# The first wide attention: the maxima's bias and mask come as bf16 tables through one product, and VectorE adds two key tiles for the softmax sums, whose product stands a tick later

## The reference, cut to what matters

```
q = _l2norm(q) * q_scale
k = _l2norm(k) * k_scale
sim = jnp.einsum('bhid,bhjd->bhij', q, k) * ATTN_SCALE
...
sim = sim + dist[None, None] * slopes[None, :, None, None]
...
sim = jnp.where(causal_mask[None, None], neg, sim)
attn = jax.nn.softmax(sim, axis=-1)
out = jnp.einsum('bhij,bhjd->bhid', attn, v)
...
return out @ w_out
```

## Time and profile before

| | us |
|---|---|
| three runs | 2496.67, 2497.49, 2497.55 |
| median | 2497.49 |
| the profiled execution | 2501.75 |
| its span in the profile | 2500.1 |
| TensorE busy in the span | 2348.6 (94%) |
| VectorE busy | 1606.9 (64%) |
| ScalarE busy | 1484.6 (59%) |
| GpSimd busy | 1588.9 (64%) |
| transfers, mean | 33 GB/s |

### The profile page before, as it was taken

One profiled execution on the slowest core, in us unless ns is written; L12 is line 12 of the kernel. 1 busy time (PEld: TensorE's weight loads), 2 busy tenths in 40 slices (PEclk: granted clock), 3 DMA queues, 4 the chain that ended last, 5 costly groups with the idle time before them and its releaser, 6 DMA issues. The chain is left out here.

```text
span 2500.1 us, 61330 instructions
## 1 busy us (share of the span) xinstructions
PE 2348.6 (94%) x23721; PEld 1826.3 (73%) x23721; DVE 1606.9 (64%) x4042; ACT 1484.6 (59%) x2974; POOL 1588.9 (64%) x2537
## 2 busy tenths in 40 slices
PE   6999999999999999988999999999999968799997
PEld 5888888888886556656777787787877757566665
DVE  5666666666664578874445477777777733378786
ACT  5666666666664478864444466666666523377774
POOL 6888888888885364443333277777777732367663
PEclk9999999999999989999999999999999979899999
DMA  8940000000000010001000000000000036100000
GB/s 293 331 142 2 2 2 2 2 2 2 2 2 1 1 47 2 2 2 33 1 1 1 3 4 4 6 6 4 6 6 4 6 100 183 55 10 10 8 4 34
DMA packets 22915, 82.90 MB, mean 33 GB/s; under 512 B 3970, under 2 KB 10883, under 8 KB 21603
## 3 DMA queue, kind: packets, MB, share of 16 engines
q1 hardware_dynamic: 19474, 71.76, 8.9%
q0 software_dynamic: 3152, 7.21, 0.9%
HBM read 71.76 MB, written 46.79 MB: 47 GB/s over the span
## 5 line engine op out<-in xcount | busy, mean ns | idle before, releaser
L978 POOL TENSOR_TENSOR XR<-XR,T 128x256 f32<-128x256 f32 x504 | 368.9, 732 | 36.9 <-DVE T L858 7.3
L722 ACT ACTIVATE P<-ps 128x384 f32<-128x384 f32 (+1 forms) x512 | 250.7, 542 | 179.5 <-PE ps L2755 178.1
L2755 PE MATMUL ps<-P,V 128*64 128x256 f32 (+3 forms) x4096 | 335.0, 349 | 0.8 <-ACT P L722 0.7
L1523 DVE TENSOR_REDUCE bm<-ps 128x3 f32<-128x384 f32 x512 | 260.6, 551 | 54.4 <-PE ps L2755 52.0
L2755 PEld LDWEIGHTS ps<-P,V 128*64 128x64 f32 (+1 forms) x4096 | 186.1, 124 | 123.6 <-issue 47.0
L1463 ACT ACTIVATE P<-ps 128x768 f32<-128x768 f32 x256 | 207.7, 811 | 75.6 <-PE ps L2755 70.3
L889 DVE TENSOR_REDUCE sm<-ps 128x2 f32<-128x512 f32 (+1 forms) x256 | 130.0, 549 | 188.0 <-PE ps L2755 188.0
L1630 POOL TENSOR_SCALAR_AFFINE_SELECT P<-P 128x512 f32<-128x512 f32 x256 | 165.5, 647 | 103.6 <-ACT P L1463 102.0
L991 POOL TENSOR_TENSOR PS<-P 128x256 f32<-128x256 f32 x256 | 181.4, 734 | 70.8 <-ACT P L722 70.5
L2755 PE MATMUL ps<-mk,identb 128*128 128x256 bf16 (+1 forms) x1024 | 204.7, 291 | 12.7 <-DVE bm L1523 8.9
L1012 POOL TENSOR_TENSOR ss<-ss,nhalf 128x16 f32<-128x16 f32 x64 | 188.0, 2938 | 5.3
(11 more groups left out here) (315 smaller groups left out, 6838.5 us busy)
## 6 DMA issues: line engine op xcount, KB each, us to landing
rows_i<-in_zero SPq DMA_DIRECT2D x16, 1208.0 KB, 31.1
rows_o<-in_zero SPq DMA_DIRECT2D x16, 1208.0 KB, 80.9
w<-in_m_w SPq DMA_DIRECT2D x23, 578.0 KB, 4.0
zt<-rows_i SPq DMA_DIRECT2D x23, 128.0 KB, 3.1
rows_o<-yo POOLq DMA_DIRECT2D x23, 128.0 KB, 3.9
stg<-in_t_w SPq DMA_DIRECT2D x11, 256.0 KB, 2.8
XR<-in_x SPq DMA_DIRECT2D x4, 512.0 KB, 9.4
out<-XR SPq DMA_DIRECT2D x8, 256.0 KB, 2.0
```

The source lines that it names most:

```text
L722: e.activation(self.P[at % 6][:, :], K.ps.ap("st", s, g, h)[:, 0:self.w], ACT.Exp, bias=0.0, scale=1.0 if kind == 0 else 0.125).then_inc(K ...
L978: p = po.e.tensor_tensor(x, x, self.T[g % 2][:, par, pr], ALU.add)
L1523: e.tensor_reduce(bm[:, h, :], K.ps.ap("mx", s, g, h)[:, 0:384].rearrange("p (a c) -> p a c", c=128), X, ALU.max, negate=True).then_inc(K. ...
L2755: return self.te.matmul(o, l, r, start=start, stop=True, skip_group_check=True)
```

## The change

Maxima: the table bt holds, for each head, the linear bias of 256 keys in bf16, with the mask already added for the second 128. TensorE multiplies it with the identity (identb) as the first product into each mx bank, in the mask's place: for the second query tile (n = 0) over all 512 columns of the bank instead of 256, for the first tile (n = 1) over 256 as before. The four fp32r bias products of each n are gone. As the bias is counted for the second query tile, VectorE adds 128 times the slope (s128) to four of the eight maxima, one small instruction before L901. The bias in the exponentials stays exact; the maximum cancels in the softmax.

Sums: VectorE adds the two key tiles' exponentials of the second query tile, P[:,128:256] + P[:,256:384], into PS (four instructions of 128x128 a unit, two in the tick behind each half of st). TensorE then multiplies ones with 128 columns of P and with 128 columns of PS for each head, at its own step sm, which comes a tick behind pv; sT and out move a tick later, and a unit has 25 ticks instead of 24.

Start: the bias chunks KB are copied by ScalarE behind ticks 5 and 7 of the first unit instead of all ahead of tick 2, the chunk for on is gone, the null values' product moves from tick 8 to 12, and a transfer of 1 MB brings bt behind the first two chunks.

```diff
-            first, last, unit = 8, 13, 24
-            self.tk = {"qk": 0, "turn": 6, "mx": 9, "v": 12, "mT": 15, "st": 17, "pv": 20, "sT": 21, "out": 22}
+            first, last, unit = 8, 13, 25
+            self.tk = {"qk": 0, "turn": 6, "mx": 9, "v": 12, "mT": 15, "st": 17, "pv": 20, "sm": 21, "sT": 22, "out": 23}
...
-        for ps in mx:
-            o = ps[:, 0:2 * w].rearrange("p (a c) -> p a c", a=2)[:, :, w - 128:w]
-            K.acc(o, K.identb[:, :], K.mk[:, 0, :].unsqueeze(1).to_broadcast([128, 2, 128]), start=True)
+        if mx:
+            pe.wait_ge(self.bt_in, 16)
+        for par, ps in enumerate(mx):
+            at = 512 * (g_mx % 4) + 256 * par
+            bt = self.bt[:, at:at + 256].bitcast(BF16)
+            if n:
+                K.acc(ps[:, 0:256].rearrange("p (a c) -> p a c", a=2), K.identb[:, :],
+                      bt.rearrange("p (a c) -> p a c", a=2)[:, :, 128:256], start=True)
+            else:
+                K.acc(ps[:, :], K.identb[:, :], bt, start=True)
...
-        for pr in range(2):
-            for par in range(2):
-                r = slice(64 * par, 64 * par + 64)
-                p = K.acc(ps[par][:, w * pr:w * pr + w], self.on[r, :], KB[r, 2 * u + pr, 0:w])
...
-        if kind == 0:
-            for kt, q, c, w in self.blocks():
-                for h in range(4):
-                    p = K.acc(sm[32 * h:32 * h + 32, q:q + w], self.one[:, 0:32], P[h][:, c:c + w], start=kt == 0)
-            p.then_inc(K.ps.full_of("sm", s, g), 1)
...
+            if self.kind == 0:
+                K.acc(sm[r, 0:128], self.one[:, 0:32], self.P[(4 * g + h) % 6][:, 0:128], start=True)
...
+        for h in range(4 if self.kind == 0 else 0):
+            p = K.acc(sm[32 * h:32 * h + 32, 128:256], self.one[:, 0:32], self.PS[g % 2][:, h, :])
...
+        n = self.part("st", k - 1)
+        if kind == 0 and n is not None:
+            if g >= 2:
+                dv.wait_ge(*K.ps.filled("sm", s, g - 2))
+            for h in (2 * n, 2 * n + 1):
+                P = self.P[(4 * g + h) % 6]
+                dv.wait_ge(*K.ps.read("st", s, g, h))
+                e.tensor_tensor(self.PS[g % 2][:, h, :], P[:, 128:256], P[:, 256:384], ALU.add).then_inc(self.halved, 1)
...
+        dv.after(dv.step(e.tensor_tensor(sm[:, 0:4], sm[:, 0:4], K.pc("s128", 4 * (g % 4), 4), ALU.add)))
```

More of the change, by code:

```diff
@@ L181, in __init__ @@
             self.raw = [sb(f"raw{s}_{i}", [128, 512], F32) for i in range(6)]
+            self.PS = [sb(f"PS{s}_{i}", [128, 4, 128], F32) for i in range(2)]
+            self.halved = K.sem(f"halved{s}")
             self.sqr = [sb(f"sqr{s}_{i}", [128, 512], F32) for i in range(3)]
@@ L466, in pe_scores @@
         if self.kind == 0:
[L467 removed]
+            self.pe_masks(pe, st, mx, n, g_mx)
         if st:
@@ L480, in pe_scores, with pe_masks @@
                 self.pe_mx2(mx, g_mx, n)
-    def pe_masks(self, pe, st, mx, n):
-        K, w = self.K, 128 if n else 256
+    def pe_masks(self, pe, st, mx, n, g_mx):
+        K = self.K
         pe.wait_ge(K.masks_in, 2)
@@ L568, in pe_halves @@
         for h in range(4):
-            p = K.acc(sm[32 * h:32 * h + 32, 0:256], self.one[:, 0:32], self.PS[g % 2][:, h, :], start=True)
+            r = slice(32 * h, 32 * h + 32)
+            if self.kind == 0:
+                K.acc(sm[r, 0:128], self.one[:, 0:32], self.P[(4 * g + h) % 6][:, 0:128], start=True)
+            else:
+                p = K.acc(sm[r, 0:256], self.one[:, 0:32], self.PS[g % 2][:, h, :], start=True)
+        for h in range(4 if self.kind == 0 else 0):
+            p = K.acc(sm[32 * h:32 * h + 32, 128:256], self.one[:, 0:32], self.PS[g % 2][:, h, :])
         p.then_inc(K.ps.full_of("sm", s, g), 1)
@@ L614, in act, with act_kb @@
             elif name == "unit":
-                if a == (0, 0) and k == 2:
-                    self.act_kb(ac)
-                if self.kind == 0 and a == (0, 0) and k == 8:
+                if self.kind == 2 and a == (0, 0) and k == 2:
+                    self.act_kb(ac, 0, 1)
+                if self.kind == 0 and a == (0, 0) and k == 12:
                     self.act_nvw(ac)
                 self.act_unit(ac, *a, k)
+                if self.kind == 0 and a == (0, 0) and k in (5, 7):
+                    self.act_kb(ac, k - 5, k - 3)
             elif name == "load":
                 a[0].act(ac, k)
-    def act_kb(self, ac):
+    def act_kb(self, ac, lo, hi):
         K, kind, e = self.K, self.kind, ac.e
-        for c in range(5 if kind == 0 else 1):
+        for c in range(lo, hi):
             n = self.kb_at + c
@@ L731, in act_unit @@
                          ACT.Copy).then_inc(K.ps.out_of("pv", s, g), 1)
-        if self.part("pv" if kind == 0 else "sm", k) is not None:
-            if kind == 2 and g >= 2:
+        if self.part("sm", k) is not None:
+            if g >= 2:
                 ac.wait_ge(*K.ps.filled("sT", s, g - 2))
@@ L1040, in sp @@
         if self.kind == 0:
-            for c in range(5):
-                n, w = self.kb_at + c, 512 if c < 4 else 128
-                K.sp_stage(sp, n, K.stg[n % 2][:, 0:w], K.t["kb0"][:, 512 * c:512 * c + w])
+            for c in range(4):
+                n = self.kb_at + c
+                if c == 2:
+                    sp.e.dma_start(self.bt[:, :], K.t["bt"]).then_inc(self.bt_in, 16)
+                K.sp_stage(sp, n, K.stg[n % 2][:, :], K.t["kb0"][:, 512 * c:512 * c + 512])
             K.sp_stage(sp, self.nvs_at, K.stg[self.nvs_at % 2][:, :], K.t["nvs"])
@@ L2997, in lay_out @@
         "rev": np.broadcast_to(np.arange(8, 0, -1), (128, 8)),
+        "s128": np.broadcast_to(128 * slopes.reshape(4, 2, 2).transpose(0, 2, 1).reshape(1, 16), (128, 16)),
             }
```

32 lines of the change are left out of this document (15 added, 17 removed).

## The result

The changed kernel takes 2523.39 us (median of four runs, 2518.67 to 2526.55), the kernel before, on the same chip, 2497.52 (2496.67 to 2501.96): a ratio of 1.0094, 95% interval 1.0079 to 1.0108, so it is slower by 0.8 to 1.1%. The profiled execution had 2518.67, with a span of 2517.0.

A forecast was written before the change was run, and what follows sets the result against it. TensorE, busy 99.5% in the steady stretch, was taken as the bound. A 12.6, B 12.8, C and D 22.3 gave 47.7 a round against 46.93; 15 rounds, less 1.5 at the start, add 10 us: 2507, range 2484 to 2525.

The forecast's parts named there:

- C and D together: Two periods of a round where TensorE's own work hides VectorE's chain: forecast to fall from 23.50 to 22.3 us.
- TensorE saves 0.6 a period: TensorE, each period: bias products save 0.33 and 0.22, sums 0.26, the table costs 0.2; net 0.6 us, 2.4 a round.
- the prediction's own 11.15 for TensorE in A: Period A: TensorE's own length before the change, 11.42 less a wait of some 0.27 us; 10.55 forecast after it.
- VectorE's chain, A 11.95 without the port: VectorE from maxima to T and hand-over, 10.5 us, plus 1.45 for first z and statistics: A 11.95 without blocking by GpSimd.
- The port, 0.65 in A and 0.3 in B: VectorE instructions with two SBUF inputs meeting GpSimd's additions onto XR: 0.65 us charged in A, 0.3 in B.
- B 12.8: Period B: second query tile's maxima start at 4.1, giving 12.5 us, plus 0.3 for meetings with GpSimd; 12.01 before.
- Start, 1.5 gained: First unit: spreading the bias chunks ScalarE copies gives back 0 to 3 us, taken as 1.5.
- Rounds: Steady part of the first stage: a round of four periods 47.7 against 46.93 us, 0.77 longer, 15 times 11.6.
- the one where the port costs nothing: Rival: GpSimd's additions fall elsewhere and block nothing; A 11.95, B 12.6, C and D 22.3, around 2491 us; chance 0.25.
- That T is not the last wait: Rival: TensorE stays the bound, saving 3.1 a round, 47 us, with a time of 2449 us; chance 0.07.
- The third, a blocked link of the minima each time: Rival: VectorE's minima chain and second add wait for GpSimd additions; 1.6 a round, 24 us, time 2531; chance 0.13.
- The fourth, the power: Rival: GpSimd's power also blocks VectorE's adds ahead of KL; each period waits 2 us more, time 2600; chance 0.02.

## Why the prediction was nearly right, point by point

The sign, the mechanism and the periods that lose were as predicted: TensorE's busy share fell to 94.5%, and its waits name T's line. The number was 16 us low, near the upper end of the range: A was put 0.81 too long, B 0.68 too short, C and D together 0.77 too short. That the first error has the other sign is luck. With A right and all else as forecast, the sum would have been 12 us lower, about 2495 (an estimate: 0.81 times 15 rounds), and would not have said slower.

- *TensorE saves 0.6 a period.* This is the step that failed in size: it saves 0.22. The bias products are gone as counted (0.33 and 0.22), but mask and table of the second query tile take 0.22 more (411.67 to 412.43, 0.76 instead of 0.54; I had 0.2), and the four KH x QH products that now stand directly ahead of the wA products take 0.38 instead of 0.29, so the table gives 0.25. The sums' product fell from 0.79 to 0.57, 0.22 as against 0.26, and the later tick costs 0.25, a term that I did not have: I priced each product by its own rows and not by its neighbours. C and D took 23.07, not 22.3. With 0.22 in place of 0.6 the prediction's own 11.15 for TensorE in A becomes 10.93; the version without z in A has 10.94.
- *VectorE's chain, A 11.95 without the port.* Right within 0.16. The maxima came at 4.85 (416.52 less 411.67; I said 4.76), the pair took 0.46 to 0.54 (0.5), T ended 0.14 ahead of the mask product. A is 11.79.
- *The port, 0.65 in A and 0.3 in B.* The meeting exists, but I had the place wrong. In A almost nothing is lost, because the pair comes 0.18 before a GpSimd addition ends and the last of the four ends at 417.61, so that L910 (417.41) takes 0.22 and not 0.51 as in C. In B 0.95 is lost: 0.48 on the second z, which I had said would no longer meet an addition onto XR, and 0.47 on the pair. And it works both ways, GpSimd is held up as well, which I did not count.
- *B 12.8.* It is 13.48. Besides the port, z starts 3.33 behind the mask product that opens B, so the maxima start at 4.96 and not at 4.1. I kept GpSimd's part at its old place although its additions and a longer A move it.
- *Start, 1.5 gained.* Not seen: the first T comes 1.7 later. With the table alone it comes 0.2 earlier, with the later tick and no additions 1.3 later; but between versions that differ only in GpSimd's roots it moves by over 1 us (69.61 and 70.83), so this is not shown to be the change's. Another 2.8 come in the last eleven units, where the clock falls to 1.2 GHz for 3.41 us from 746.15; before, it does not fall there.
- *Rounds.* 1.45 a round instead of 0.77; the twelve rounds measured make 17.4 of the 22.7.

Of the rivals, the one where the port costs nothing is out in B and nearly right in A. That T is not the last wait is out: it is the last in A and B, though in C and D TensorE is, as forecast. The third, a blocked link of the minima each time, is seen only in C, where L910 takes 0.51 and nobody waits for it; its time, 2531, is near for another reason. The fourth, the power, is out: the Trainium skill, "SBUF — State Buffer", section "Who interferes with whom", would have the pair at 421.00 blocked for the whole of the power, which runs from 419.89 to 422.94; it took 0.46, so the rule does not hold for this power. For additions and normalisations of GpSimd the trace agrees: an addition of VectorE that meets one ends 0.15 behind its end, 0.77 instead of 0.28 at 430.21 and 1.13 each beside the two normalisations of the version with additions behind T.

What stays open: why the power takes 3.05 in A of the changed kernel, why the clock falls after one wait of TensorE and not after another of the same length, and what in TensorE makes the neighbours cost; I saw where, not why.

## What to carry to other kernels

Where one engine is busy 99%, ask for each period which chain on the other engines ends how far ahead of it: here VectorE's ended A already, and a change that put two pairs of 0.5 each into it lost more than TensorE gained. Price a product together with its neighbours; moving it by one place cost as much as the shorter product saved. And look for the wait that swallows a gain first: two short roots that stood behind 2 us of independent work hid two thirds of what the table saves, and moving them was worth 0.3% in the kernel before and some 1.3% in the changed one (1.0094 against 0.9966).

## What the runs showed of the hardware

- An addition of 128x128 with two SBUF inputs on VectorE takes 0.28 alone. One that begins during a GpSimd addition or multiplication ends 0.15 behind it: 0.33 to 0.85 beside additions of 128x256, 1.13 beside a multiplication of 128x512; the GpSimd instruction is held too (0.86 instead of 0.73, 2.21 instead of 2.04 for two). As a reduction with one input it takes 0.40 to 0.42, beside GpSimd's additions too.
- It is not held by a GpSimd power of 128x16: 0.26 to 0.29 inside 2.93 to 3.05.
- On TensorE, P x one begins 0.21 behind the start of the last wA product, a mask product or transpose 0.12; transposes 0.31 behind that of the half-height score products, the output product 0.23.
- The granted clock fell to 1.2 GHz for over 3 us behind a wait of 1.14 (once 1.35) in three of twelve rounds of one kernel, behind waits of 0.91 and 1.21 in half the rounds of another, and never, from 100 to 700 us, in two others whose longest single waits were 1.2 (additions as reductions; first z behind T).
